# GpSimd instead of VectorE makes the low parts of the dense layers' weights, in a four-layer graph network kernel

## The reference

```
h = relu(layernorm(x));  x = x + L0(h)   # layer 0: sparse attention, 8 heads; then ln, silu(z @ W1 + b1) @ W2 + b2
h = relu(layernorm(x));  x = x + L1(h)   # layer 1: mean over neighbours @ W_l.T + b_l + h @ W_r.T, batch norm, relu, + h
h = relu(layernorm(x));  x = x + L2(h)   # layer 2: relu(gcn(h, W1, b1)), relu(gcn(h, W2, b2))
h = relu(layernorm(x));  x = x + L3(h)   # layer 3: (1 + eps) h + sum over neighbours; relu(@ W1.T + b1) @ W2.T + b2; layer norm
return x
```

## Time and profile before

| what | value |
|---|---|
| time, median of 3 runs | 395.43 us |
| lowest and highest run | 393.89 and 395.63 us |
| span of the profiled execution | 394.1 us |
| PE, DVE, ACT, POOL busy | 374.8, 312.1, 171.6, 4.2 us |
| low parts of weights on DVE (line 652) | 24 instructions, 29.1 us |
| DMA, mean | 84 GB/s |

### The profile page before, as it was taken

How to read it: one execution, slowest core, us unless ns; L and a number is a source line. 1 busy time by engine, 2 the same in 40 slices (tenths; PEclk the granted TensorE clock), 3 DMA queues, 4 the chain that set the end, 5 groups by cost and what they waited for, 6 DMA issues and landing times.

```text
span 394.1 us, 5108 instructions
## 1 busy us (share of the span) xinstructions
PE 374.8 (95%) x1786; PEld 282.2 (72%) x1786; DVE 312.1 (79%) x660; ACT 171.6 (44%) x287; POOL 4.2 (1%) x19
## 2 busy tenths in 40 slices
PE   2989999999999999999999999999999999999994
PEld 1545566666657888887678788887588878787773
DVE  5889999999848789897868976698875788388236
ACT  5664666563044234244559533262363530145410
POOL 4000000000000000000000000000000000000000
PEclk9999999999999999999999999999999999999988
DMA  7602444343135000068200512200600050000002
GB/s 238 250 1 69 152 154 141 105 153 112 52 112 183 1 2 0 2 215 315 111 2 1 172 43 101 114 0 0 211 4 0 2 180 33 2 0 0 2 12 94
DMA packets 16360, 32.92 MB, mean 84 GB/s; under 512 B 1360, under 2 KB 1488, under 8 KB 16336
## 3 DMA queue, kind: packets, MB, share of 16 engines
q1 hardware_dynamic: 15744, 32.25, 23.9%
q10 hardware_dynamic: 592, 0.36, 0.3%
HBM read 21.07 MB, written 1.05 MB: 56 GB/s over the span
## 4 chain that ended last, share of the span: by engine, by line
PE 77%; DVE 14%; ACT 4%; issue 2%; DMA 1%; DVEq 0%; ACTq 0%
PE acc L1395 11%; PE bank L1377 10%; PE bank L1480 7%; PE bank L1270 6%; PE bank L1271 6%; PE bank L1251 4%; PE acc L1251 4%; PE acc L1271 4%; PE acc L1270 4%; PE bank L1465 3%; PE acc L1451 3%; DVE big_rounded L652 2%; PE acc L1228 2%; PE bank L1228 2%; PE acc L1545 2%
## 5 line engine op out<-in xcount | busy, mean ns | idle before, releaser
L1395 PE MATMUL acc<-wide_rounded,c_rounded 128*126 128x512 f32 x200 | 59.5, 439 | 0.7 <-ACT acc L464 0.7
L1395 PEld LDWEIGHTS acc<-wide_rounded,c_rounded 128*126 128x126 f32 x200 | 36.9, 186 | 19.8 <-issue 13.0
L792 DVE TENSOR_SCALAR wide_rounded<-iota_f,picked 128x512 fp32r<-128x512 f32 x100 | 42.2, 480 | 1.5 <-issue 1.1
L483 ACT COPY z_sb<-acc 126x512 f32<-126x512 f32 x37 | 21.6, 585 | 42.0 <-PE acc L1395 33.3
L507 ACT ACTIVATE wide<-wide,low_col 128x512 f32<-128x512 f32 x32 | 21.3, 715 | 32.9 <-DVE low_col L905 32.8
L1480 PEld LDWEIGHTS bank<-v_sb,big 128*128 128x128 f32 x256 | 29.7, 192 | 4.7 <-issue 4.0
L625 DVE TENSOR_TENSOR wslot_rounded<-wslot,wide_rounded 128x512 fp32r<-128x512 f32 x24 | 16.2, 687 | 21.2 <-ACT wslot L377 21.2
L1480 PE MATMUL bank<-v_sb,big 128*128 128x65 f32 x256 | 31.6, 277 | 0.0
L798 DVE TENSOR_TENSOR c_rounded<-row_bc,wslot_rounded 128x1008 fp32r<-128x1008 bf16 x25 | 30.0, 1201 | 0.0
L1377 PE MATMUL bank<-t_sb,wslot 128*128 128x512 f32 x64 | 29.5, 594 | 0.5 <-ACT t_sb L459 0.5
L652 DVE TENSOR_TENSOR big_rounded<-big,big_rounded 128x1024 fp32r<-128x1024 f32 x24 | 29.1, 1221 | 0.5
(11 more groups left out here) (312 smaller groups left out, 769.6 us busy)
## 6 DMA issues: line engine op xcount, KB each, us to landing
big<-z_sb SPq DMA_DIRECT2D x36, 252.0 KB
big<-in_w SPq DMA_DIRECT2D x4, 2048.0 KB, 7.8
x_sb<-in_x SPq DMA_DIRECT2D x8, 256.0 KB, 4.6
big<-in_w_3t SPq DMA_DIRECT2D x2, 1024.0 KB, 6.7
row_bc<-in_rows SPq DMA_DIRECT2D x7, 256.0 KB, 6.4
wslot<-in_wq SPq DMA_DIRECT2D x1, 1024.0 KB, 8.9
wslot<-in_wk SPq DMA_DIRECT2D x1, 1024.0 KB, 10.7
wslot<-in_wv SPq DMA_DIRECT2D x1, 1024.0 KB, 12.8
```

Of the source, the lines that this page charges most:

```text
L483: nc.scalar.copy(stage[0:BROWS, b % STAGES, :], a).then_inc(S["staged"], 1)
L792: nc.vector.tensor_scalar(hot_ring[:, u, k, :], iota_f[:, :], picked[:, 0, s0 + k:s0 + k + 1], None, ALU.is_equal)
L1395: last = nc.tensor.matmul(to, st_ring[:, u, 2 * k + a, :, :].rearrange("p w k -> p (w k)"), hot_ring[:, u, k, :], start=False, stop=False, ...
```

## The change

`weight_lo` moves from VectorE's block to the end of GpSimd's, and all 24 calls with it. The instruction, its operands and its semaphores are the same; the waits for `<name>_hi` stand on GpSimd now. On GpSimd the 24 follow one another in the order in which VectorE had them; nothing else stands in its list there. VectorE keeps its `weight_hi` calls.

```
+            for name in ("w1_0", "w2_0"):
+                for q in range(4):
+                    weight_lo(name, q, q + 1)
+            for after, q in enumerate((2, 3, 0, 1)):
+                weight_lo("w_lr", q, after + 1)
+            for name in ("w1_2", "w2_2", "w_3"):
+                for q in range(4):
+                    weight_lo(name, q, q + 1)
...
-            for q in range(3):
-                weight_lo("w1_0", q, q + 1)
             for t in range(NT):
                 split_lo("ff_in", t, t_lo, t_at, ready=("t_ready", NT))
-            weight_lo("w1_0", 3, 4)
...
-                elif f < 6:
-                    weight_lo("w2_0", f - 2, f - 1)
...
-                    weight_lo("w_lr", t + 1, t)
...
-                weight_lo("w_lr", q, q + 3)
...
-            weight_lo("w1_2", 0, 1)
-            weight_lo("w1_2", 1, 2)
             bn_coefs(0)
-            weight_lo("w1_2", 2, 3)
             bn_coefs(1)
...
-            weight_lo("w1_2", 3, 4)
...
-                    weight_lo("w2_2", f // 2, f // 2 + 1)
...
-                weight_lo("w_3", q, q + 1)
```

More of the change, by code:

```diff
@@ L357, in _, with weight_lo @@
                            allow_small_or_imprecise_dtypes=True).then_inc(S["tables"], 1)
+            def weight_lo(name, q, after):
+                part = slice(q * FT // 4, (q + 1) * FT // 4)
+                lo, hi = weights[name]
+                pool.wait_ge(S[name + "_hi"], after)
+                nc.gpsimd.tensor_tensor(lo.rounded[:, part, :], lo.full[:, part, :], hi.rounded[:, part, :].bitcast(F32),
+                                        ALU.subtract).then_inc(S[name + "_lo"], 1)
+            for name in ("w1_0", "w2_0"):
[6 more added lines that the diff above has]
+                    weight_lo(name, q, q + 1)
         @block.scalar
@@ L645, in weight_hi @@
                 nc.vector.tensor_copy(hi.rounded[:, part, :], lo.full[:, part, :]).then_inc(S[name + "_hi"], 1)
[L647 to L653, removed]
             def moments(t, source, done):
```

## The result

The changed kernel takes 412.3 us (median of 5 runs, 410.46 to 412.51) against 395.43 (393.89 to 395.63): ratio 1.043, 95% interval 1.0405 to 1.046. It is slower by 4.3%, forecast was 409.6, 3.6%. After's profile has a span of 409.0, its other four runs 410.8 to 411.0, so like against like is 410.8 - 394.1 = 16.7 us.

What follows compares the result with a forecast made beforehand. TensorE, busy 95% of the span, was taken as the bound. Terms 4.4 + 2.8 + 6.6 + 0.4 = 14.2 us on a span of 394.1 gave 408.3; with the median 1.3 above the span, 409.6. Range: 394.6 to 414.

Steps and rivals of the forecast that it cites:

- d: Time of one low part on GpSimd, taken as 2.3 us from the select's 0.29 us for 128 columns.
- The pessimistic end, 3.9: Upper bound for one low part on GpSimd, scaled from the index table: 3.9 us, giving 429 us; chance 0.05.
- Two-input instructions on VectorE are held: VectorE instructions with two SBUF inputs wait out each whole GpSimd low part; 404 to 413 us, chance 0.47.
- Layer 0's norm: Ahead of layer 0's W1, VectorE's norm, held by GpSimd's four w1_0 low parts, ends 4.4 us later; bounds 0 and 6.7.
- Layer 0's W2: VectorE's additions and splits beside GpSimd's w2_0 low parts start TensorE's next tile 2.8 us later; bounds -0.36 and 5.5.
- Layer 1's splits of h1: Not counted separately: layer 1's other low parts meet slack, at most 2.3 us each where VectorE waits anyway.
- Ahead of the batch norm: In layer 1, VectorE's work and GpSimd's 9.2 us make line 1053 start 6.6 us later; bounds 0 and 7.
- `w2_2`, 0.4: In layer 2, w2_2's last low part comes late and starts TensorE's matmul some 0.4 us later.
- The clock: TensorE's clock may halve behind new idle times in layer 0's norm and layer 1: up to 3.2 us, outside the sum.
- Freeing VectorE: Gain from taking the low parts off VectorE: 0.4 us, of which 0.36 at layer 0's W2 and 0.04 in layer 1.
- only copies held: Rival: GpSimd holds VectorE's copy-like instructions, not two-input ones: 398.8 us; chance 0.24, shared with stages held in part.
- nothing held: Rival: GpSimd holds no VectorE instruction that matters: 395.4 us, not slower; chance 0.22.

Runs made afterwards that it cites:

- run 5: The changed kernel with GpSimd's 24 subtractions replaced by fills with zeros, which read nothing (result lacks the weights' low parts): 393.94 us, ratio 0.999 to the kernel before.
- run 6: The changed kernel with GpSimd copying the high part into the low part's place, one input (result wrong): 394.72 us, ratio 0.999 to the kernel before.
- run 1: The kernel before with only layer 0's eight low parts (w1_0, w2_0) moved to GpSimd: 400.29 us, ratio 1.016.
- run 2: Also called the layer-1 kernel: the kernel before with only the eight low parts of w_lr and w1_2 moved to GpSimd: 403.15 us, ratio 1.023.
- Run 3: The kernel before with only the eight low parts of w2_2 and w_3 moved to GpSimd: 395.93 us, ratio 1.0026.
- run 10: The changed kernel plus 24 unread matmuls in TensorE's 6.4 us idle time ahead of the batch norm's transposes: 409.94 us, ratio 1.039 to the kernel before.
- run 4: The changed kernel with no low parts made; GpSimd only passes semaphores and TensorE reads high parts instead: 393.16 us, ratio 0.997 to the kernel before.
- run 7: The changed kernel with each low part cut into four GpSimd instructions of 128x256: 412.27 us, ratio 1.045 to the kernel before.
- run 8: The changed kernel with GpSimd starting w1_0's low parts only after layer 0's norm has ended: 406.36 us, ratio 1.030 to the kernel before.
- run 9: The kernel before with the 12 high parts of w_lr, w2_2 and w_3 copied by GpSimd, VectorE keeping all low parts: 394.75 us, ratio 1.002.

## Why the prediction was right, and where its terms were off

Point by point, against the 16.7 us of like against like (the milestones give 16.4):

- **d, one low part on GpSimd**, 2.3 us: 2.35 to 2.41 alone, up to 2.87 where GpSimd itself was held. The select of rows 3, scaled by columns, was the right neighbour. The pessimistic end, 3.9, was far off.
- **Two-input instructions on VectorE are held**, which no row of before showed: right, in the last fences of after and in runs 5 and 6. The rule that the prediction took from the Trainium skill (SBUF — State Buffer, Who interferes with whom), that a two-input VectorE instruction contends with a GpSimd instruction that reads SBUF, is borne out: 0.69 beside a fill, 1.41 beside a one-input copy, 2.8 beside a subtraction.
- **Layer 0's norm, 4.4**: 4.0. The idle time and PSUM work counted as cover was about right.
- **Layer 0's W2, 2.8**: 2.1. The sum put the end of VectorE's last split at 227.8 without the norm's 4.0; it is at 231.9.
- **Layer 1's splits of h1, "slack", 0**: wrong by 1.4. The step that failed is the sentence that layer 1's other lows meet slack. The two splits take 1.97 and 1.98 (0.69 unheld). Runs 1 and 2 each show no wait at the fourth tile, so the slack is there in either alone. What I missed is the lateness that VectorE brings out of W2. It reaches the first tile's statistics 9.1 later than the layer-1 kernel (236.78 against 227.67), TensorE its first product of h1 only 7.1 later (248.86 against 241.73), so 2.0 of the slack is gone.
- **Ahead of the batch norm, 6.6**: 6.2 to 6.4. In run 2 alone the first statistics are at 274.62, 5.9 later than before.
- **`w2_2`, 0.4**: by the milestones 0.2 between layer 1's third statistics and this matmul. Run 3, where `w2_2` and `w_3` are alone on GpSimd, has ratio 1.0026, that is 1.0 us, with an interval from 0.3 to 1.8; in its trace TensorE waits 0.35 for that low part.
- **The clock, 0 to 3.2 and left out of the sum**: 2.3. It fell at both places named. In layer 0 the 16 highs take 5.51 for 3.96, of which 0.7 reaches the end; in layer 1 it is the 1.6 of run 10. The prediction named this term and its places but put it at nothing in the likeliest time; it should have had it, since the sum itself makes TensorE stand idle at both places (2.15 and 6.4 us measured).
- **Freeing VectorE, 0.4**: run 4 bounds it at 0.3%, 1.1 us, with an interval from 0.4 to 1.9.

So the terms that were in the sum measured 4.0 + 2.1 + 6.4 + 0.2 = 12.7 for 14.2, and two that were not, 1.4 and 2.3, make up for it (16.4, against 16.7 by the spans). The mechanism and the places are as forecast; that the time came within 0.7% is in part luck, since 1.5 too much in the counted terms met 3.7 left out. The rivals fall with line 1010 at 2.79 (only copies held: 0.69) and with the norm at 2.58 (nothing held: 0.55).

## What to carry to other kernels

An engine's low load is no reason to move work to it: ask first what the work costs where it is (here one wait of 0.2 us), then price the new instruction and everything on VectorE with two SBUF inputs, or like a copy, that falls beside it, both times one behind the other. A GpSimd instruction of about 1.1 us in place of a VectorE one of 1.22 was free here; one of 2.35 cost 4%. Cutting it into pieces shortens each wait and lengthens the sum. And slack counted for each stage by itself has been spent once two of them are late.

## What the runs showed of the hardware that was not expected

GpSimd is held too. Its 128x256 pieces took 3.28 / 4 = 0.82 us each at 242.30 and 17.78 / 16 = 1.11 between VectorE's instructions; in these stretches the two engines go in turn, one instruction each. Cutting a 128x1024 subtraction into four costs 3.28 against 2.41 with nothing beside it.

A 128x1 instruction with two SBUF operands is held like a 128x512 one, until the GpSimd instruction ends (line 676, 1.85 for 0.16, from 188.15 to 190.00).

TensorE's clock drops late in the program in some profiles and not in others. Before's profile shows 0.83 in the ten microseconds from 374 on, run 5's shows 1.00 there (start:end, length, busy times of PE, PEld, DVE, ACT, POOL, granted clock, DMA share, GB/s). Before:

```profile
374.00:384.00 10.00, 10.00 (x36) 7.77 (x37) 4.00 (x8) 1.56 (x3) 0.00 (x0) 0.83 0.01 4
```

Run 5:

```profile
374.00:384.00 10.00, 10.00 (x44) 7.98 (x44) 5.79 (x12) 1.23 (x4) 0.00 (x0) 1.00 0.07 26
```

Eight fewer matmuls fit into the same stretch. The drop comes 2 to 4 us after the start of the eight matmuls that use one row, with no idle time of TensorE, in the profiles of before and of runs 2, 3 and 4; behind the same eight there is none in those of after and of runs 1 and 5 to 10. From the first of the eight to the first low matmul of the second tile behind them it is 7.4 us in before (373.93 to 381.34) and 5.8 in run 5 (373.27 to 379.07), 1.6 less. That the runs of one kernel differ by the same thing is inferred from their times, since each kernel has one profile. What decides it was not tried.

The drop behind 6.4 us of idle time came each time: the granted clock is 0.50 from 284 to 288 in the changed kernel, and runs 2, 7 and 8 have it behind waits of 6.38, 5.76 and 6.38. Filling 5.35 us of it with matmuls that nobody reads kept the clock at 1.00. Behind the wait of 2.15 in layer 0's norm the clock fell in all three profiles looked at (changed kernel, runs 1 and 10), but not at the same place.
